# Seven bank addresses and a count loaded into eight registers at once, where one packed word was loaded and unpacked

## What is computed

```
h = jnp.maximum(_layernorm(x, axis=-1), 0.0)
deg = jnp.maximum(segment_sum(ones, dst), 1.0)
tmp = res = h
for i in range(3):
    tmp = tmp + segment_sum(tmp[src], dst) / deg[:, None]
    res = res + tmp / (1.0 + i)
x = x + res
```

## Time and profile before

| what | us |
|---|---|
| median of 3 runs | 2225.24 (2220.71 to 2227.39) |
| the profiled execution | 2225.23 |
| its span, first to last instruction | 2223.4 |
| VectorE's first one-hot to the first product of the aggregation | 66.25 to 358.14 |

### The profile page before, as it was taken

One profiled execution on the slowest core, in us unless ns is written; L12 is line 12 of the kernel. 1 busy time (PEld: TensorE's weight loads), 2 busy tenths in 40 slices (PEclk: granted clock), 3 DMA queues, 4 the chain that ended last, 5 costly groups with the idle time before them and its releaser, 6 DMA issues.

```text
span 2223.4 us, 38121 instructions
## 1 busy us (share of the span) xinstructions
PE 1696.1 (76%) x8603; PEld 1278.4 (57%) x8603; DVE 1793.9 (81%) x5310; ACT 1113.9 (50%) x2933; POOL 860.3 (39%) x861
## 2 busy tenths in 40 slices
PE   3677777998999998734677787777657878887886
PEld 2222224877887887523577676666635555555554
DVE  8988887999999896886877877877577777778775
ACT  1766665887887884300234333243544444444442
POOL 3000000000000000067777777772037777777771
PEclk9765667999999999867688788798868788777877
DMA  6355556765665666055656566663112222222221
GB/s 211 105 153 149 149 149 205 279 221 185 243 247 207 249 245 229 7 170 152 176 159 186 162 167 184 169 177 99 47 52 55 55 56 55 55 55 53 56 55 41
DMA packets 192477, 314.96 MB, mean 142 GB/s; under 512 B 25873, under 2 KB 139416, under 8 KB 182418
## 3 DMA queue, kind: packets, MB, share of 16 engines
q1 hardware_dynamic: 163312, 248.12, 34.2%
q0 software_dynamic: 27712, 63.56, 11.0%
q10 hardware_dynamic: 1250, 0.86, 0.1%
HBM read 232.38 MB, written 80.07 MB: 141 GB/s over the span
## 4 chain that ended last, share of the span: by engine, by line
POOL 23%; PE 14%; issue 12%; DVE 12%; DMA 4%; ACT 1%; SPq 1%; DVEq 1%; POOLq 0%; ACTq 0%
POOL G L701 11%; POOL G L686 7%; POOL SCR L686 5%; PE PS L2035 3%; PE PS L1928 2%; PE PS L1929 2%; PE PS L1818 1%; DVE HOT_R L1185 1%; PE PS L1904 1%; DMA G<-table,src_idx 1%; DVE RX L1621 1%; DMA gathered_rows<-G 1%; DMA SCR<-table,src_idx 1%; PE PS L1778 1%; DVE GROUPED_R L1200 1%
## 5 line engine op out<-in xcount | busy, mean ns | idle before, releaser
L686 POOL DMA_INDIRECT G<-table,src_idx x252 | 265.2, 1052 | 983.3 <-DMA table<-RX 904.3
L701 POOL DMA_INDIRECT G<-table,gather_idx x415 | 407.3, 981 | 252.4 <-DMA table<-RX 126.2
L2035 PE MATMUL PS<-SCR,OH 128*128 128x256 f32 x830 | 286.1, 511 | 102.6 <-DVE SCR L1658 99.6
L2035 PEld LDWEIGHTS PS<-SCR,OH 128*128 128x128 f32 x830 | 203.7, 255 | 155.9 <-DVE SCR L1658 114.6
L1818 PE MATMUL PS<-ALL_R 128*128 128x256 f32 (+3 forms) x2025 | 266.5, 288 | 19.7 <-DVE ALL_R L1248 9.0
L1904 PE MATMUL PS<-RX,OH 128*128 x830 | 173.6, 364 | 139.4 <-DVE SCR L1360 87.6
L1818 PEld LDWEIGHTS PS<-ALL_R 128*128 128x128 f32 (+1 forms) x2025 | 251.3, 191 | 22.7 <-DVE ALL_R L1248 9.4
L1904 PEld LDWEIGHTS PS<-RX,OH 128*128 128x128 f32 x830 | 144.8, 239 | 169.5 <-issue 164.2
L1928 PE MATMUL PS<-AT 128*128 128x128 f32 x830 | 208.4, 338 | 18.9 <-issue 9.8
L1766 PE MATMUL PS<-AT,G 128*128 128x400 bf16 x474 | 170.3, 465 | 68.6 <-DVE AT L1141 52.1
L1778 PE MATMUL PS<-HOT_R,GROUPED_R 128*119 128x448 f32 x830 | 193.6, 380 | 15.4 <-DVE G L1206 15.3
(11 more groups left out here) (396 smaller groups left out, 3411.3 us busy)
## 6 DMA issues: line engine op xcount, KB each, us to landing
ALL_R<-adjacency SPq DMA_DIRECT2D x72, 1600.0 KB, 6.8
adjacency<-ALL_R SPq DMA_DIRECT2D x26, 1600.0 KB, 7.4
AT<-gathered_rows SPq DMA_DIRECT2D x103, 256.0 KB, 3.7
gathered_rows<-G SPq DMA_DIRECT2D x63, 256.0 KB, 2.3
AT<-dst_in_block SPq DMA_DIRECT2D x103, 128.0 KB, 3.9
gathered_rows<-SCR SPq DMA_DIRECT2D x40, 256.0 KB, 2.3
G<-table,gather_idx POOLq DMA_INDIRECT x415, 2.5
G<-table,src_idx POOLq DMA_INDIRECT x252
```

The source lines that it names most:

```text
L686: pool.indirect_dma_start(score_rows(i)[:, q], None, tables[0], bass.IndirectOffsetOnAxis(ap=src_idx[:, v:v + 1], axis=0)).then_inc(s(f"sc ...
L701: pool.indirect_dma_start(G[:, p, q, :], None, tables[i], bass.IndirectOffsetOnAxis(ap=gather_idx[:, p, q:q + 1], axis=0)).then_inc(s(f"{n ...
L2035: ins = pe.matmul(PS[:, q, 0:MSG], OH[:, p, q, :], view(SCR, M_AT + (p * VB + q) * MSG, [[1, MSG]]), start=True, stop=True)
```

## The change

The packed word goes. VectorE writes, for each of the 85 words, a row of eight integers: seven bank addresses (bank number times 512) and the count plus one. The rows lie in the second half of `begins`, which the one-hots' ring uses only up to its first 800 elements. TensorE loads the row into eight registers with one instruction, without a check of the bounds, and uses seven of them as addresses. The eighth still goes through one mask before the wait, which bounds its value. `pair_words` moves to the start of its row.

```
-        bank_words = AT[0:1, 17, 0:AB].bitcast(I32)
-        pair_words = AT[0:1, 17, AB:AB + SLOTS // 2].bitcast(I32)
+        pair_words = AT[0:1, 17, 0:SLOTS // 2].bitcast(I32)
+        BANK_W = AV + 1
+        bank_words = begins[0:1, 2 * NT + 602:2 * NT + 602 + AB * BANK_W].bitcast(I32)
...
-            done(dve.tensor_scalar(bank_words, view(HB, 1200 + AV - 1, [[AV, AB]], 1).bitcast(I32), ROOM_BIT, None, ALU.logical_shift_left))
-            for q in range(AV):
-                to = some
-                done(dve.tensor_scalar(to, view(HB, 1200 + q, [[AV, AB]], 1).bitcast(I32), BANKS - 1, 3 * q, ALU.bitwise_and, ALU.logical_shift_left))
-                done(dve.tensor_tensor(bank_words, bank_words, some, ALU.bitwise_or))
+            addresses = view(begins, 2 * NT + 602, [[BANK_W, AB], [1, AV]], 1).bitcast(I32)
+            done(dve.tensor_scalar(addresses, subs.rearrange("o (k q) -> o k q", q=AV), BANKS - 1, 9, ALU.bitwise_and, ALU.logical_shift_left))
+            done(dve.tensor_scalar(view(begins, 2 * NT + 602 + AV, [[BANK_W, AB]], 1).bitcast(I32), view(HB, 1200 + AV - 1, [[AV, AB]], 1).bitcast(I32), 1, None, ALU.add))
...
-                word = pe.value_load(bank_words[0:1, k:k + 1], min_val=0, max_val=(SLOTS << ROOM_BIT) - 1)
-                pe.wait_ge(s("banks_zeroed"), (word >> ROOM_BIT) + 1)
+                _, words = nc.values_load_multi_w_load_instructions(bank_words[0:1, k * BANK_W:(k + 1) * BANK_W], engines=[mybir.EngineType.PE], min_val=0, max_val=(BANKS - 1) * 512,
+                                                                    skip_runtime_bounds_check_because="a masked and shifted bank number, or the count of a slot")
+                pe.wait_ge(s("banks_zeroed"), words[AV] & 255)
...
-                    pe.matmul(PSF[:, bass.ds(((word >> (3 * q)) & (BANKS - 1)) << 9, KEYS)], src_hot(v), key_hot(v), start=False, stop=False,
+                    pe.matmul(PSF[:, bass.ds(words[q], KEYS)], src_hot(v), key_hot(v), start=False, stop=False,
```

More of the change, by code:

```diff
@@ L245, in gnn_program @@
         last_of_tile = HB[0:1, NT:2 * NT]
-        bank_words = AT[0:1, 17, 0:AB].bitcast(I32)
-        pair_words = AT[0:1, 17, AB:AB + SLOTS // 2].bitcast(I32)
+        pair_words = AT[0:1, 17, 0:SLOTS // 2].bitcast(I32)
+        BANK_W = AV + 1
+        bank_words = begins[0:1, 2 * NT + 602:2 * NT + 602 + AB * BANK_W].bitcast(I32)
+        assert 2 * NT + 602 + AB * BANK_W <= 4 * NT + 600 and (HOTS - 16) * KEYS // 2 <= 2 * NT + 602 and BANK_W % 4 == 0
         WIDE = (RING * PER_BLK + OVER) * SUBW
```

## The result

| kernel | median, us | runs | range |
|---|---|---|---|
| before | 2225.14 | 10 | 2219.93 to 2230.92 |
| changed | 2211.63 | 10 | 2206.64 to 2217.70 |

The ratio is 0.9938, with a 95% interval of 0.9923 to 0.9954: 13.5 us less. The forecast was 2212.

A forecast was written before the change was run, and what follows sets the result against it. TensorE's sequencer was taken to bound the build at 11.06 us a block, the store ring close behind. Gains of 0.6 + 2.8 + 8.5 + 1.5 = 13.4 us off 2225.2 gave 2212 us, range 2205 to 2232.

The forecast's parts named there:

- The sequencer: TensorE's instruction issue in the build stage, said to set the pace before the change at 11.06 us a block.
- the ring: Build-stage store buffers: a later pair's copy waits for a block's store to land; said to bind after the change.
- The ring's period: Time from store to store in the build: at least 10.5 us, put at 10.6 with slower stores.
- The waits: Sign: ScalarE's copies wait on stores 30 us or more in about 20, from 11.6 in 7; on TensorE under 80.6.
- The load of eight registers: TensorE's load at each word, taken as twice the single load: 0.6 us in quiet, 1.8 inside a store.
- rival 1: At each of 85 words the load grows with its registers: slower, 2235 to 2390 us, chance 0.15.
- 153 us of sequencer time: TensorE work removed at visits and words: 85 x 7 visits x 0.2 plus 85 x 0.4 us.
- TensorE after the change: TensorE's own time in the build's middle: 10.2 us a block, closely under the ring's 10.6.
- The 80% for blocks with many visits: Middle of the build: of 10.6 us possible gain only 80% counted, 8.5 us, as TensorE has little slack.
- rival 4: Inside words the matmul, not registers, sets 0.33 us; only word gaps shrink, 0.4 us; chance 0.56 together with the forecast.
- The set-up: VectorE's packing before the build: 3.3 us come free, 0.6 us counted as gain, bounds 0 and 3.3.
- The first ten pairs and the end: Build's start, bound by VectorE's 0.40 us a visit, gains 2.8 us; its last steps and pairs gain 1.5.

The follow-up runs named there:

- the late zeroing: First pair of each block zeroed behind the second pair's copy: kernel before 2522.20 us against 2524.09 unedited; changed kernel 2490.53 us.
- half stores: Only the first 64 of 128 partitions of each adjacency block stored and fetched: kernel before 10.94 us a block, changed kernel 9.54.
- the two edits: Changed kernel with the late zeroing and ScalarE's word for each block's second pair loaded before the store wait: 2487.51 us against 2532.90 before.

## Why the prediction was right, point by point

- **What bounded the kernel before.** The sequencer, with the ring just behind it: shown by the late zeroing, which gave nothing before the change and 12.7 us of the stage after it, and by the check's removal, which alone took 0.4 us off a block. The half stores, which shortened the landing by 1.1 us, gave only 0.12 us a block before.
- **The ring's period.** 10.6 forecast, 10.64 measured. The waits moved as forecast, but less through the rows that name the store: 22.1 us in 9 instead of 30 in about 20, because the trace puts most of them down to TensorE, as it did at 201.01.
- **The load of eight registers.** 0.6 and 1.8 us taken, 0.59 and 1.78 measured. The reason that I gave, one contiguous row, was incomplete: the row's start decides, as the rows of nine show. With one integer more in each row rival 1 comes true in kind, at +0.6% and not +7%. The rows off that start cost (1.935 - 0.304) / 7 = 0.23 us for each further register, the aligned ones (0.591 - 0.304) / 7 = 0.04. The Trainium skill's rule ("Runtime: NRT & Kernel Launch", "Instruction fetch mechanics"), some 200 ns for each register even in bulk, comes near the first and does not hold for the second, where the measurement decides.
- **What was removed.** The prediction counts 153 us of sequencer time and says that the ring takes most of it back. The loads, twice as long, took back a third of it first: 97.9 us where they took 47.4. The sum for TensorE had the longer loads in it, the 153 us did not.
- **TensorE after the change.** 10.2 us a block was too high; it is at most 9.67, in the kernel with the two edits. Part of it is the clock: the sum was weighted with 0.65, and the middle of that kernel (89.3 to 311.8) was granted 0.75, with which the same sum gives an estimated 9.8. Which other term was too high, no run shows. The 80% for blocks with many visits was too careful: all of the 0.42 us was gained, 9.7 us where I counted 8.5. Weight loads stood as close as 0.11 us, which rules out rival 4.
- **The set-up.** 0.6 us forecast, none measured. VectorE's two instructions took 1.1 us instead of 4.4, as priced, but all of it was lost at the next wait for ScalarE, and the first one-hot came at 66.72, 0.5 us later than before:

```profile
61.53 0.32 DVE L973 RECIPROCAL small<-small 128x25 f32<-128x25 f32 x1 [6.70 <-ACT small L716]
...
66.72 0.25 DVE L1140 TENSOR_SCALAR G<-iota_h,OH 128x128 bf16<-128x128 int16 x1
```

- **The first ten pairs and the end.** From the first one-hot to the first store it is 24.9 us instead of 28.0, 3.1 gained where 2.8 were forecast; less the 0.5 us of the set-up that is 2.6, where 3.4 were forecast for both. 2.0 at the end, 1.5 forecast. VectorE's own steps did not hide wholly: its line 1164 ended at 343.76, ScalarE's last copy at 343.73. The sum is 14.3 against 13.4. The errors of the parts are small and of both signs, so the closeness of the total, 2211.6 to 2212, is partly luck: a measurement of this kernel scatters by more.

## What to carry to other kernels

When the bound is an engine's sequencer, price what stands next before pricing what is removed: here an estimated 153 us of register work went, 50 us came back as longer loads, and 14 us were gained. The check alone shortened the stage by 12 us and the total by 8. A ring of buffers has a period of its own, the landing plus all that its owner does until the next store, and it is shortened by moving work of the owner out of that piece (a zeroing, a load of an address). An engine that starts the moment a transfer lands is not proof that the transfer is the bound: here 15 of 22 did so in a kernel where a shorter ring gave nothing. Load several registers with one instruction only from rows that start at a multiple of 16 bytes.

## What the runs showed of the hardware

- A register load from SBUF takes 0.30 us for one register and 0.59 for eight in an aligned row of 32 bytes, but 1.94 for the same eight from rows that do not start at a multiple of 16 bytes.
- While a store of 1.6 MB from SBUF to HBM runs, each of these takes about three times as long: 0.92, 1.78 and up to 5.96 us. With a store of half the partitions it is no less: 1.06 and 2.06 us in the median.
- A store of 64 partitions with the same bytes in each takes 6.3 us to land, one of 128 partitions 7.4, both in the median.
